# A Mamba-2 layer and a ternary feed-forward layer on one core: passage between token blocks reordered, TensorE's program written out, low halves of three heads' weights on GpSimd

## The reference, cut to what matters

```python
# 2 sequences x 2048 tokens x 512 features, all float32
def mamba(u):                                   # 8 heads of 128, state 64, chunks of 64 in the reference
    z, xBC, dt = split(u @ W_in.T)              # 1024, 1152, 8 columns
    dt = softplus(dt + dt_bias)
    xBC = silu(causal_conv(xBC, conv_w, width=4) + conv_b)
    x, B, C = split(xBC)
    y = selective_scan(x, dt, -exp(A_log), B, C) + x * D
    yg = y * silu(z)
    return (yg * rsqrt(mean(yg * yg) + 1e-5) * norm_w) @ W_out.T
x = layernorm(u + mamba(u))
wu, wg, wd = (ternary(w) for w in (W_up, W_gate, W_down))   # sign or 0 by mean(|w|), times that mean
out = layernorm(x + (silu(x @ wu.T) * (x @ wg.T)) @ wd.T)   # hidden 2048
```

## Time and profile before

| | |
|---|---|
| median of 3 runs | 1370.12 us (1369.99 to 1370.62) |
| the profiled execution, its own time | 1370.94 us |
| its span (first to last instruction) | 1369.2 us |
| mean granted clock of PE | 0.996 of full |
| busy: PE, DVE, ACT, POOL | 1333.5, 1041.0, 784.3, 650.3 us |

### The profile page before, as it was taken

How to read it: one execution, slowest core, us unless ns; L and a number is a source line. 1 busy time by engine, 2 the same in 40 slices (tenths; PEclk the granted TensorE clock), 3 DMA queues, 4 the chain that set the end, 5 groups by cost and what they waited for, 6 DMA issues and landing times.

```text
span 1369.2 us, 26933 instructions
## 1 busy us (share of the span) xinstructions
PE 1333.5 (97%) x9318; PEld 866.4 (63%) x9318; DVE 1041.0 (76%) x1857; ACT 784.3 (57%) x1561; POOL 650.3 (47%) x634
## 2 busy tenths in 40 slices
PE   7899999999999999999999999999999999999998
PEld 4455565655555646556556677777777767777774
DVE  7887887887878868788684877777777767777775
ACT  6796673874757828658474555454544545454441
POOL 0575364673755837536255534353443424353331
PEclk9899999999999999999999999999999999999999
DMA  8537334353442633424546332223122322222002
GB/s 245 167 132 228 131 110 116 89 160 101 126 127 82 174 88 99 150 86 147 142 115 214 88 118 56 72 63 85 48 62 67 74 68 56 73 62 55 32 25 69
DMA packets 162796, 143.83 MB, mean 105 GB/s; under 512 B 101344, under 2 KB 123232, under 8 KB 161504
## 3 DMA queue, kind: packets, MB, share of 16 engines
q1 hardware_dynamic: 162656, 142.05, 36.1%
HBM read 99.93 MB, written 27.39 MB: 93 GB/s over the span
## 4 chain that ended last, share of the span: by engine, by line
PE 80%; DVE 7%; issue 4%; DMA 3%; ACT 2%; POOL 2%; SPq 1%; POOLq 0%; DVEq 0%; ACTq 0%
PE ring L936 20%; PE ring L1151 15%; PE ring L965 8%; PE p_turn L1131 7%; PE p_y L1131 7%; PE p_st L1131 6%; PE p_seg L1131 5%; PE p_y L1009 3%; PE p_y L1017 2%; PE p_st L999 2%; DMA quant<-in_w_ffn 2%; PE p_turn L989 1%; DVE acc L1804 1%; PE ring L1188 1%; DVE abs_sum L1782 1%
## 5 line engine op out<-in xcount | busy, mean ns | idle before, releaser
L936 PE MATMUL ring<-u_split,weights 128*128 128x512 f16 x1620 | 375.0, 382 | 2.2 <-DVE x_ch L1809 2.0
L936 PEld LDWEIGHTS ring<-u_split,weights 128*128 128x128 f16 x1620 | 154.9, 99 | 171.9 <-issue 6.6
L1713 POOL TENSOR_TENSOR xdt<-xdt 128x512 f32<-128x512 f32 x64 | 100.6, 1571 | 340.0 <-DVE xdt L2175 340.0
L965 PE MATMUL ring<-w_out,raw 128*128 128x512 f16 x672 | 147.3, 379 | 0.2 <-issue 0.2
L1804 DVE SCALAR_TENSOR_TENSOR acc<-ring,taps,acc 128x511 f32<-128x511 f32 (+2 forms) x192 | 143.7, 749 | 4.5
L965 PEld LDWEIGHTS ring<-w_out,raw 128*128 128x128 f16 x672 | 65.7, 98 | 79.5 <-issue 0.7
L1359 ACT ACTIVATE xdt<-p_turn,dts 128x128 f32<-128x128 f32 x256 | 72.7, 375 | 70.3 <-PE p_turn L989 70.3
L1620 POOL TENSOR_TENSOR raw<-yg,raw 128x512 f16<-128x512 f32 x64 | 78.8, 1231 | 65.9 <-ACT raw L1389 65.8
L1615 POOL TENSOR_TENSOR yg<-y_ch,z_ch 128x512 f32<-128x512 f32 x64 | 81.4, 1273 | 41.4 <-DVE y_ch L1929 41.4
L1368 ACT ACTIVATE p_seg<-cum_rows,cum 128x128 f32<-128x128 f32 x256 | 80.8, 389 | 8.7 <-DVE seg L1907 8.7
L1591 POOL TENSOR_TENSOR rstd<-var_e,exponent 128x1 f32<-128x1 f32 x32 | 20.2, 631 | 118.4 <-DVE var_e L1952 118.4
(11 more groups left out here) (395 smaller groups left out, 3246.7 us busy)
## 6 DMA issues: line engine op xcount, KB each, us to landing
cum_rows<-cum_dram SPq DMA_DIRECT2D x64, 256.0 KB, 4.1
quant<-in_w_ffn SPq DMA_DIRECT2D x24, 512.0 KB, 4.4
quant<-in_w_ffn SPq DMA_DIRECT2D x48, 256.0 KB, 4.1
cum_g<-cum_dram SPq DMA_DIRECT2D x64, 128.0 KB, 4.4
rows<-in_u_tok SPq DMA_DIRECT2D x32, 256.0 KB, 4.5
x_dram<-rows SPq DMA_DIRECT2D x32, 256.0 KB, 2.1
tern_ug<-quant SPq DMA_DIRECT2D x32, 256.0 KB, 3.3
u_raw<-in_u_t SPq DMA_DIRECT2D x7, 1024.0 KB, 8.7
```

The lines of the kernel that those rows point to most:

```text
L936: mm = pe.matmul(bank_k[:, :], w_in[:, ws, k, col:col + P], us[:, par, k * T:(k + 1) * T], start=(i == 0), stop=(i == 3 * KD - 1))
L965: mm = pe.matmul(ring[b][:, :], ys[:, h, c * P:(c + 1) * P], w_out[:, ws, h, :], start=(h == 0 and ys is y_hi and ws == 0), stop=(h == H - ...
L1713: pool.tensor_tensor(tile_[:, 1, :, :], tile_[:, 0, :, :], tile_[:, 1, :, :], ALU.mult).then_inc(hid_ok, 1)
```

## The change

- PE's two loops are replaced by straight code for all blocks (`for n in range(NB): step(n, n % 2)` and the same for the feed-forward part); the other engines keep theirs.
- The low halves of heads 2, 3 and 7 are made on POOL by `w_lo_head` in two instructions each (multiply by SW in place, subtract the high half), behind the high half of their piece. DVE makes those of the small piece, heads 0 and 1, heads 4 and 5 together, and head 6 later. Waits on w_lo_ok and w_half_ok follow.
- In the opening DVE makes b before c and c after the next convolution; in place 2 of block 0 it has an order of its own (`second_slot`), with carry, B and C, and the states ahead of the convolution; ACT does tanh of B and C, the second transposed x and the logarithm of dt ahead of head 4's tanh.
- The odd rows of the magnitudes move back by one place (`odd_rows`); SP loads the second output weights ahead of rows 4 and 5 and a cumulative sum ahead of row 13.
- In block 7, SP issues two parts' transposes before the first store and load of a chunk, then two, then one; DVE takes residuals ahead of splits.
- After block 7: product 5 of the first pair ahead of product 6; ACT reads u3 and the next s1 between the last gates; POOL's root ahead of a hidden product; chunk 3's residual in place 7 instead of 6; residuals 0 and 3 ahead of the sum c12; at t = -1 DVE's first `hidden` ahead of the splits.

```diff
+POOL_HEADS = [2, 3, 7]
 def head_weights(h):
-    return 1 + h if h < 2 else 2 + h // 2
+    return 2 + h if h < 2 else 2 + h // 2
...
+        def raw_head(h):
+            return raw_piece(head_piece(h))[:, :, 2 * P * (h % 2):2 * P * (h % 2 + 1)]
+        def odd_rows(n, p, when):
+            rows_ = {(0, 3): (5, 7), (1, 0): (9, 11), (1, 1): (13, 15, 17, 19), (1, 2): (21, 23)}
...
         def attention_rest(t, q):
-            return {2: 0, 3: 1, 4: 2, 6: 3}.get(q) if is_at(t, -1) else None
+            return {2: 0, 3: 1, 4: 2, 7: 3}.get(q) if is_at(t, -1) else None
...
                         load_cum(0, 0, 1)
-                        sp.wait_ge(w_lo_ok, 4)
+                        sp.wait_ge(w_lo_ok, 3)
+                        sp.wait_ge(w_half_ok, 2)
                         load_abs(0)
...
                             if is_at(n, NB - 1):
-                                for j in range(4):
+                                for j in range(2):
                                     turn_x(0, 0, j)
                             store_x1(n - 1, 0)
                             load_utok(n - 1, 2)
                             if is_at(n, NB - 1):
-                                turn_x(0, 0, 4)
+                                for j in range(2, 4):
+                                    turn_x(0, 0, j)
                             store_x1(n - 1, 1)
                             load_utok(n - 1, 3)
+                            if is_at(n, NB - 1):
+                                turn_x(0, 0, 4)
...
                     if is_at(n, 0) and p == 2:
+                        load_wout(1)
                         load_abs(4)
                         load_abs(5)
-                        load_wout(1)
...
             def head_tile(n, par, kind, h):
-                if is_at(n, 0) and h == 2:
-                    pe.wait_ge(w_half_ok, 1)
+                if is_at(n, 0) and h in POOL_HEADS:
+                    pe.wait_ge(w_half_ok, POOL_HEADS.index(h) + 1)
                 elif is_at(n, 0):
-                    pe.wait_ge(w_lo_ok, head_weights(h) + 1)
+                    pe.wait_ge(w_lo_ok, head_weights(h))
...
             def turn_b(n, use):
-                wait_apart(pe, bc_ok, n * 3 + 3, passed["pe"])
+                wait_apart(pe, bc_ok, n * 3 + 1, passed["pe"])
...
             def cb(n, par, use):
                 pe.wait_ge(turn_free, use)
+                wait_apart(pe, bc_ok, n * 3 + 3, passed["pe"])
...
-            run_steps(pe, step)
+            for n in range(NB):
+                step(n, n % 2)
...
             product(0, 0, 0, 1, True)
+            pe.wait_ge(turn_free, turn_use(NB, "x01") + 1)
+            product(0, 0, 0, 5, True)
             pe.wait_ge(s1_ok, 1)
             product(0, 0, 0, 6, False)
-            pe.wait_ge(turn_free, turn_use(NB, "x01") + 1)
-            product(0, 0, 0, 5, True)
...
-            ffn_steps(pe, ffn_step)
+            ffn_step(-1, 1)
+            for t in range(NB):
+                ffn_step(t, t % 2)
...
         @block.scalar
...
+                    if is_at(n, 0) and p == 2:
+                        cb_tanh(1, ring[ring_bank("cb", 0)])
+                        x_dt(n, par, p, 1)
                         conv_in(n, 2 * p)
-                    if state_slot(n, p):
+                        decays(n, par, p, 1)
+                        dt_ln(1)
+                    elif not end:
+                        conv_in(n, 2 * p)
...
             chain_read(0, 0, u2, prod[6], u2_ok, c12_ok)
             gated(NB, 0, 1)
+            chain_read(0, 0, u3, prod[7], u3_ok, c21_ok)
             act.wait_ge(scales_ok, 3)
             gated(NB, 1, 0)
+            chain_read(0, 1, s1, prod[1], s1_ok, c11_ok)
             gated(NB, 1, 1)
...
         @block.gpsimd
...
+            def w_lo_head(h):
+                own, k = raw_head(h), POOL_HEADS.index(h)
+                pool.wait_ge(w_hi_ok, head_piece(h) + 1)
+                pool.tensor_scalar(own, own, SW, None, ALU.mult).then_inc(w_mul_ok, 1)
+                pool.wait_ge(w_mul_ok, k + 1)
+                pool.tensor_tensor(w_in[:, 1, :, 2 * P * h:2 * P * (h + 1)], own, w_in[:, 0, :, 2 * P * h:2 * P * (h + 1)],
+                                   ALU.subtract).then_inc(w_half_ok, 1)
...
+            w_lo_head(2)
+            w_lo_head(3)
             b_decay(0, 0, 0, turn_use(0, "b0"))
             c_decay(0, 0, 1)
             b_decay(0, 0, 1, None)
             wout_scale(0)
+            w_lo_head(7)
             wout_low(0)
...
                         m, its, k = before
-                        hidden(m, k, True)
                         if is_at(t, -1) and q == 2:
                             pool.wait_ge(ms_ok, 1)
                             pool.tensor_tensor(rms[:, :], ms[:, :], exponent[:, :], ALU.pow).then_inc(rms_ok, 1)
+                        if attention_rest(t, q) == 3:
+                            norm_root(NB - 1, 3)
+                        hidden(m, k, True)
                         hidden(m, k, False)
...
         @block.vector
...
             cum_turned(0, turn_use(0, "cumt0"))
-            w_lo_head(2, w_half_ok)
-            cb_silu(0, 0, p_y[0])
+            cb_silu(0, 0, p_y[0], False)
             z_gate(0, 0)
-            w_lo_head(3, w_lo_ok)
+            conv(0, 0, 1)
             b_read(0, 0, turn_use(0, "b0"))
-            conv(0, 0, 1)
+            c_silu(0, 0, p_y[0])
...
+            magnitude(1)
             w_lo(4)
-            magnitude(1)
-            w_lo(5)
-            cb_conv(1, 1, ring[ring_bank("cb", 0)])
-            dt_second(1)
+            def second_slot():
+                n, par, p = 0, 0, 2
+                skip(n, p, 0)
+                skip(n, p, 1)
+                state_update(n, par, p - 1, C - 1)
+                cb_conv(1, 1, ring[ring_bank("cb", 0)])
+                dt_sum(1)
+                within(n, par, p, 0)
+                cb_silu(1, 1, ring[ring_bank("cb", 0)])
+                dt_inverse(1)
+                for c in range(C - 1):
+                    state_update(n, par, p, c)
+                within(n, par, p, 1)
+                conv(n, par, 2 * p)
+                b_read(1, 1, turn_use(0, "b"))
+                dt_third(1, 1)
+                silu(n, 2 * p)
+                z_gate(n, 2 * p)
+                cum_read(1, 1, turn_use(0, "cum"))
+                w_lo_head(6)
+                conv(n, par, 2 * p + 1)
+                silu(n, 2 * p + 1)
+                magnitude(3)
...
                         residual(n - 1, 0, ring[ring_bank("chunk", 0)])
+                        normalise(n - 1, 0)
+                        residual(n - 1, 1, ring[ring_bank("chunk", 1)])
                         x_low(0, 0, 2)
                         x_low(0, 0, 3)
-                        normalise(n - 1, 0)
-                        residual(n - 1, 1, ring[ring_bank("chunk", 1)])
+                        normalise(n - 1, 1)
                         x_sum(2)
+                        residual(n - 1, 2, ring[ring_bank("chunk", 2)])
                         x_low(0, 0, 4)
-                        normalise(n - 1, 1)
-                        residual(n - 1, 2, ring[ring_bank("chunk", 2)])
+                        normalise(n - 1, 2)
                         x_sum(3)
-                        normalise(n - 1, 2)
...
                     if earlier:
                         hidden_low(*earlier, False)
+                    if attention_rest(t, q) in (0, 3):
+                        residual(NB - 1, attention_rest(t, q), p_down[attention_rest(t, q) % 2])
                     if before:
                         summed(m, k, "c12", u2, u2_ok, 5, ALU.add)
                     if has_up(t):
                         summed(n, q, "c11", s1, s1_ok, 2, ALU.add)
+                    if is_at(t, -1) and before:
+                        hidden(m, k, True)
```

More of the change, by code:

```diff
@@ L1474, in step @@
                         split_u(n + 1, 1 - par)
-                    if p == 2 and more(n):
+                    if p == 2 and more(n) and not is_at(n, 0):
                         dt_ln(n + 1)
@@ L1551, in ffn_step @@
                         m, its, k = before
+                    if before and not (is_at(t, -1) and q == 1):
                         wait(act, act_ok, 2 * (m * NQ + k) - 1)
```

92 lines of the change are left out of this document (54 added, 38 removed).

## The result

The changed kernel takes 1372.97 us (median of 15 runs, 1371.56 to 1375.48); the kernel before 1370.02 us (15 runs, 1369.19 to 1371.08) on the same chip. The ratio is 1.0021, with a 95% interval of 1.0014 to 1.0028: 2.95 us slower, where 10.1 us faster was forecast. The profiled execution of after took 1371.85 us, its span is 1370.1 us.

The account below looks back on a forecast made before the run. It took TensorE, busy 97% of the span, as the bound, with only idle time and slow clock recoverable. Loops 2.5 + passage 5.5 + opening 2.1 = 10.1 us, from 1370.1 to 1360.0 us; range 1357.5 to 1363.

Parts of the forecast that it names:

- the slower one: Rival, chance 0.04: GpSimd's multiplication by a constant is far slower than its neighbours; at 8 us the kernel takes 1374.0 us.
- Loops: PE's two loop returns, 0.98 and 1.63 us, vanish when its program is written out: 2.5 us gained.
- Passage: From the Mamba layer to the feed-forward layer, reordering removes PE's waits: 5.5 us gained in all.
- The carry: Passage, attention side: PE's 2.33 us wait for carry at 689.29 us goes, as DVE's residual gets its rows earlier.
- s1, c22 and the residual's wait: Passage, feed-forward side: three PE waits go by reordering, gaining 0.69, 1.37 and 1.54 us.
- The moved residual: Passage: chunk 3's residual one step later delays c12 on DVE; loss 0.4 us, bounds gain 0.6 and loss 1.2.
- The wait for c12: Passage: product 5 waits about 1.2 us for this DVE sum, behind chunk 3's residual and its statistics.
- Opening: First stretch of the kernel: 12.2 us of waits and slow tiles go, new costs come, 2.1 us gained net.
- (a): Opening: ACT's early logarithm of dt brings two table loads, so the next pair's transposed x waits: 2.6 us lost.
- (b): Opening: with DVE out of the way, PE meets steps that ACT paces: 1.5 us lost in small waits.
- (d): Opening: GpSimd's first multiplication and subtraction hold DVE's small dt instructions, so da and PE's cumulative sum come 4.2 us late.
- (c): Opening: GpSimd holds DVE instructions reading SBUF alone, the split of u and low halves of heads 4 and 5: 1.8 us.

Follow-up runs that it names:

- the last residual late: Changed kernel with odd rows back in their old places, last token group's residual kept in the eighth pair but behind DVE's hidden steps: 1360.33 us.
- one load moved: Changed kernel, odd rows still late, with SyncE's load of row 11 placed behind row 12's and the cumulative sums' store and loads: 1365.14 us.
- last residual in the seventh pair: Changed kernel with odd rows back in their old places and the last token group's residual and root back in the seventh pair: 1361.84 us.
- the run that catches up: Changed kernel, last token group's residual behind DVE's hidden steps, rows 1 and 3 late, later odd rows caught up from block 0's last slot: 1360.20 us.

## Why the prediction was wrong

The verdict and the sign were wrong. The step that failed is in the last paragraph of the opening: "Moved magnitudes are as many as before (12 on DVE, 12 on ACT), later by one place and so behind their loads; the constants of three waits and the loads of the output weights put ahead of two others cost SyncE nothing that PE sees." The number of VectorE's instructions was counted, not the loads that wait for them. A magnitude frees half a buffer, SyncE's next load of that parity waits for it, and SyncE's queue is in order. Booked at 0, it costs 11.5 us within the change and 22.7 us by itself. The trace of before had the warning: in the queue the store of the cumulative sums goes out at 95.39 us, 0.04 us after the sixth load ended (76.04 + 19.31), and row 9 is measured at 92.89 us; ScalarE's row 8, for which row 10's load waits, ends at 94.6 us, half a microsecond behind row 9. So there was no more slack than that to move into. No rival held this mechanism either; the slower one was about GpSimd's multiplication.

With the rows put back the change gains 8.5 us (1369.93 to 1361.47), inside the range, against 10.1 forecast. Term by term:

- **Loops**, 2.5 (bounds 1.0 and 2.6): 0.2 and 0.7 measured. The releaserless idle went as said, but the other engines' returns are what PE meets next. That stood in the prediction as a reason for 0.1 us off, and it was nearly all of it. The added code was priced at nothing, and no run shows a price for it.
- **Passage**, 5.5: 4.3 measured. The carry (1.99 in the run without the passage's edits, not 2.33), s1, c22 and the residual's wait went as worked out. The moved residual cost more than the 0.4 booked: 1.50 + 0.90 + 0.85 us of waits where 1.45 stood, 1.8 us more, past the bound of 1.2. The wait for c12 was foreseen; the one for ACT behind it, 0.85, was not, nor did the 1.45 shrink.
- **Opening**, 2.1: in the changed kernel all that was to go is gone, 12.2 us by the prediction's sum, and by 74 us PE is 7.7 us ahead. (a) was right: the wait for ACT at 70.92 is 2.58, forecast 2.6. (b), booked at 1.5, shows as waits of 0.33, 0.24, 0.62, 0.41 and 0.20 us, 1.8 in all. (d), the multiplication beside dt, was booked at 4.2 and is 0.77 us in VectorE's chain, half a microsecond on PE, whose sum over da starts at 19.77 instead of 19.27. For (c), booked at 1.8, 12.2 - 2.6 - 1.8 - 0.5 leaves next to nothing, but no run separates it. So up to 74 us the opening gained far more than the 2.1 forecast. Little of it lasts: the kernel with the rows back reaches block 2's dt projection at 129.00 us, 3.15 before the 132.15 of before. Row 3 and a slow tile take some 2 us of the lead in the second slot, and waits of 1.39 and 0.86 us for VectorE stand in block 1 at 112 and 117 us; nothing was booked for either.
- **GpSimd's multiplication** takes 2.78 us for 128x1024; the nearest row had given 2.0. The start of it was read rightly: 18.32 us, forecast 18.39. The Trainium skill (GPSIMD Engine Reference, 3.1 Elementwise) has 1.03 cycles for an element where the body uses at most two ports, by which 0.9 us was estimated; the trace disagrees, by a factor of three.
- **Signs to look for.** No idle without a releaser at the returns: so it is. No wait for carry near 689, a wait for c12: so it is. dts or da of 2 us or more, the sum over da at 22 to 26, the cb tile later than 48.01: none of them; (d) was wrong, and it said how to see that. The tile at 64.49 comes earlier (55.96), as said, and in the second slot PE never waits 2 us for DVE. "Wrong if the loops' gain is missing": it is missing.

What stays open: (b) and (c) of the opening were not run alone, nor was the early logarithm of dt; their sizes above, and where the lead goes between 74 and 129 us, are read from PE's timeline, not tried. That the kernel with the rows back falls inside the range is in part luck: the passage and the loops gave 3 to 4 us less than booked, and the multiplication beside dt cost 3.7 us less than booked.

The fastest versions are the two with the rows in time and the last residual late: 1360.33 and 1360.20 us, 0.7% below the kernel before. Both beat both kernels, and neither can be told from the other.

## What to carry to other kernels

When a reader of a double buffer moves, follow the load that waits for it into its queue and list everything behind it. An in-order queue turns one late release into a delay of stores and loads that have nothing to do with it, and the engine that suffers is another one. Look in the queue of the kernel before for how soon behind the waiting load the next transfer is issued: where that is at once, there is no slack, and the waits by releaser (8.0 us for VectorE before, 64.6 after) say which engine to look at. They don't say what it costs: with 54.1 us of them (one load moved) the kernel is 4.8 us faster than before. An idle time at a loop return is worth what is left once the other engines' returns are met.

## What was not expected of the hardware

- **A hold that ends early.** One small instruction of VectorE with its inputs in SBUF was long in every execution read with GpSimd's first multiplication (dt_s or dts, 0.91 to 1.00 us instead of 0.19; ten executions, dts in eight, dt_s in two). The next ones took 0.19 us with the multiplication still running. The prediction took from a scaling of 0.96 us that GpSimd's instruction holds VectorE for its whole length; that row showed the same 0.77 us of hold, beside an instruction of 1.3 us, and so could not tell the two readings apart. What ends the hold the runs don't show. The 0.77 us are no fixed length: in the passage of the changed kernel an instruction of VectorE on 128x512 at 797.99 us takes 1.64 instead of 0.68, beside one of GpSimd of 1.27 (797.82).
- **GpSimd's multiplication by a constant** is slower for a column (2.78 us for 1024) than its subtraction of two inputs (2.13 us); the third subtraction, beside busy VectorE, took 3.83 us, and 2.55 to 3.90 in the other nine traces.
- **The clock's part in a stall.** Behind the wait of 8.99 us the tile of 12 matmuls took 3.69 us instead of 2.75, at a granted clock of 0.57 in the window of 8 us; behind a wait of 2.06 us at 783 us (last residual in the seventh pair) 8 matmuls took 1.55 instead of 1.05. Behind a wait of 2.58 us the tile at 71.39 took 2.75 us in the changed kernel; behind one of 2.59 at the same place it took 4.33 in the run that catches up. The same wait is not followed by the same clock every time.
